# Gates of the first expert stage read from DRAM rows instead of selector products, with its first blocks moved ahead of the router's decision

## The reference: a decoder of two layers

```
# first expert stage: 2 shared and 16 routed experts, all computed for all tokens
h = relu(flat @ w1 + b1)                       # 18 experts of 176 hidden units
scores = sigmoid(flat @ centroids.T) + bias    # 16 routed experts
vals, idx = top_k(scores, 4)                   # gate of each token and expert,
gating = scattered(vals) / sum                 # 0 for twelve of the sixteen
out = flat + shared(h) + sum_e gating[:, e] * (h_e @ w2_e + b2_e)

# second expert stage: 32 experts with a capacity of 40 tokens each
Xp = x[slots_token]; Y = (silu(Xp @ Wg) * (Xp @ Wu)) @ Wd; out.at[slots_token].add(Y * w)
```

## Time and profile before

| | us |
|---|---|
| median of three runs | 715.11 (706.16 to 717.93) |
| the profiled execution's own time | 711.98 |
| its span in the profile | 710.1 |
| PE busy in the span | 615.1 (87%) |
| DVE, ACT, POOL busy | 396.7, 248.7, 328.3 |
| mean granted PE clock | 0.92 of full |

### The profile page before, as it was taken

The page is one execution under the profiler, slowest core; times in us unless marked ns, Lnnn a source line. Parts: engine busy times, 40 slices in busy tenths (PEclk is TensorE's granted clock), DMA queues, the critical chain, the costliest instruction groups (busy, mean ns, idle before and its releaser), DMA issues.

```text
span 710.1 us, 14147 instructions
## 1 busy us (share of the span) xinstructions
PE 615.1 (87%) x5509; PEld 384.1 (54%) x5509; DVE 396.7 (56%) x886; ACT 248.7 (35%) x554; POOL 328.3 (46%) x434
## 2 busy tenths in 40 slices
PE   5979989994989998899985998767999987897778
PEld 3435665442546665566652565533566655365467
DVE  3345755998437666556665565533476743943231
ACT  1214542003345443334441454321555553202340
POOL 2437726895347444444431876426688852200000
PEclk8989999996799998799998799995799999899999
DMA  6299262000200000000019895046000030016301
GB/s 227 76 170 261 66 267 113 0 1 0 76 1 0 1 1 1 1 0 2 1 56 152 108 116 182 0 104 104 2 3 3 2 135 2 1 32 243 131 26 60
DMA packets 23228, 48.41 MB, mean 68 GB/s; under 512 B 2569, under 2 KB 20507, under 8 KB 21115
## 3 DMA queue, kind: packets, MB, share of 16 engines
q1 hardware_dynamic: 21867, 44.92, 25.5%
q10 hardware_dynamic: 1296, 2.58, 1.0%
HBM read 39.63 MB, written 6.55 MB: 65 GB/s over the span
## 4 chain that ended last, share of the span: by engine, by line
PE 64%; DVE 15%; DMA 7%; POOL 4%; ACT 4%; issue 4%; SPq 3%; ACTq 0%; DVEq 0%; POOLq 0%
PE PS L1134 57%; PE PS L1138 4%; DVE R L958 3%; DVE R L955 3%; DMA R<-qk_scr 2%; SPq L330 2%; DMA WT<-in_wt_s_dram 2%; DVE stats L806 2%; DVE X L811 1%; PE PS L1157 1%; POOL R L476 1%; DMA X<-in_x_dram 1%; DVE xn L821 1%; POOL rstd L427 1%; ACT R L770 1%
## 5 line engine op out<-in xcount | busy, mean ns | idle before, releaser
L1134 PE MATMUL PS<-R 128*128 128x256 f16 (+5 forms) x2072 | 207.0, 271 | 0.1
L1134 PEld LDWEIGHTS PS<-R 128*128 128x128 f16 (+4 forms) x2072 | 135.3, 105 | 83.1 <-issue 51.8
L929 DVE TENSOR_REDUCE mx<-PS 128x4 bf16<-128x512 f32 x128 | 82.5, 686 | 53.1 <-PE PS L1134 53.1
L684 ACT ACTIVATE R<-PS 128x512 f32<-128x512 f32 x128 | 69.5, 595 | 102.5 <-PE PS L1134 102.5
L1134 PE MATMUL PS<-xnT,R 128*128 128x512 f16 (+1 forms) x348 | 87.2, 391 | 6.9 <-POOL R L555 5.4
L476 POOL TENSOR_TENSOR R<-mx,causal 128x512 bf16<-128x512 bf16 x64 | 65.2, 1040 | 54.2 <-DVE mx L929 53.5
L476 POOL TENSOR_TENSOR R<-mx,R 128x512 bf16<-128x512 bf16 x64 | 65.3, 1042 | 31.9 <-DVE mx L929 28.2
L553 POOL TENSOR_TENSOR R<-R 128x256 f16<-128x256 f32 (+1 forms) x50 | 35.3, 705 | 88.3 <-ACT R L723 88.3
L1004 DVE TENSOR_TENSOR R<-R,PS 128x512 f32<-128x512 f32 (+1 forms) x50 | 34.3, 686 | 58.2 <-ACT R L742 58.2
L1134 PEld LDWEIGHTS PS<-xnT,R 128*128 128x128 f16 (+1 forms) x348 | 34.8, 101 | 39.9 <-issue 10.1
L722 ACT ACTIVATE R<-R 128x256 f16<-128x256 f32 (+1 forms) x50 | 20.6, 413 | 84.9 <-PE PS L1134 84.9
(11 more groups left out here) (201 smaller groups left out, 889.7 us busy)
## 6 DMA issues: line engine op xcount, KB each, us to landing
R<-in_experts_dram SPq DMA_DIRECT2D x6, 1536.0 KB, 7.7
R<-qk_scr SPq DMA_DIRECT2D x48, 128.0 KB, 5.7
qk_scr<-R SPq DMA_DIRECT2D x16, 256.0 KB, 4.1
R<-in_w_dram SPq DMA_DIRECT2D x1, 3200.0 KB, 18.6
R<-in_w_dram SPq DMA_DIRECT2D x1, 3168.0 KB, 11.3
R<-qk_scr SPq DMA_DIRECT2D x48, 64.0 KB
R<-in_toe_dram SPq DMA_DIRECT2D x1, 2048.0 KB, 15.1
R<-in_experts_dram SPq DMA_DIRECT2D x2, 768.0 KB, 14.6
```

Of the source, the lines that this page charges most:

```text
L684: s.activation(PTm[:, u % 4, 4 * k:4 * k + 4, :], bank(2 + (2 * u + k) % 3).rearrange("p (h q) -> p h q", h=4), ACT.Exp, scale=c["sc"]).th ...
L929: v.tensor_reduce(mx[:, t % 4, 4 * k:4 * k + 4], bank(k).rearrange("p (h k) -> p h k", h=4), AX.X, ALU.max).then_inc(S("att_mx"), 1)
L1134: return nc.tensor.matmul(o_, l, r, start=start, stop=stop)
```

## The change

What it does, part by part:

- `sel`, `g3T`, the three bf16 parts and the gate product of every block are removed. The gates, turned once into `g0T` (18 rows of 1024), are stored to a DRAM scratch, and for each block with a routed expert (all but blocks 0 and 1, so 46 of the 50 steps) SP issues one to three transfers that read one row of 512 gates and write it to as many partitions as the block has of that expert, into a ring of four (`grow`). DVE multiplies in SBUF by SBUF.
- `up(0)`, `up(1)` stand ahead of the cross keys and of the wait for the gates; the values and `up(2)` follow the transposes; `keep_busy` is gone. High and low weights of blocks 0 and 1 are made before the layer norm's split, the bias products stand at the last block of a half, the hidden blocks have a ring of four, and the `flat` additions stand one each behind the low weights of blocks 4 to 11.
- ACT's casts of `wt_s1` in cross-attention stand at `t` = 16 and 20, POOL's subtractions at 18 and 22.
- In the second expert stage `expert_down` lags by one more group, the one-hots are turned one group ahead, and `dense_rows` stands two groups behind.

```diff
-            load(sel[0:96, :].bitcast(U16), A["sel"], "sel_ready")
+            for half in range(NH):
+                ts = slice(half * HF, (half + 1) * HF)
+                sp.wait_ge(S("g0T"), half + 1)
+                sp.dma_start(g_scr[:, ts], g0T[:, ts]).then_inc(S("g_parked"), 16)
+            sp.wait_ge(S("g_parked"), 16 * NH)
+            def gates(n):
+                i = GATED[n]
+                ts = slice(i // NB0 * HF, (i // NB0 + 1) * HF)
+                if n >= 4:
+                    sp.wait_ge(S("hg"), n - 3)
+                for e, lo, hi in gate_rows(i):
+                    sp.dma_start(grow[lo:hi, n % 4, :],
+                                 g_scr[e:e + 1, ts].broadcast_to([hi - lo, HF])).then_inc(S(f"grow{n % 4}"), 16)
+            for n in range(4):
+                gates(n)
...
+            for n in range(4, len(GATED)):
+                gates(n)

@@ gpsimd @@
-            for b in range(B):
-                flat(b)
-            for i in range(NH * NB0):
+            for i in range(2):
+                block_low(i)
...
+            for i in range(2, NH * NB0):
+                block_low(i)
+                if 4 <= i < 4 + B:
+                    flat(i - 4)

@@ scalar @@
+            for i in range(2):
+                block_high(i)
...
+            block_high(2)
...
             for i in range(NH * NB0):
+                if i == 2:
+                    cross_keys()
+                    gates()
...
-                if i >= 2:
-                    act.wait_ge(S("hg"), i - 1)
+                if i >= 4:
+                    act.wait_ge(S("hg16"), i - 3)

@@ vector @@
-                dve.wait_ge(S("gate_ps"), i + 1)
-                v.tensor_tensor(hg[0:m, i % 2, :], hid[0:m, i % 2, :], bank(2 + i % 2, parts=m),
-                                ALU.mult).then_inc(S("hg"), 1)
+                if i in GATED:
+                    n = GATED.index(i)
+                    dve.wait_ge(S(f"grow{n % 4}"), gates_loaded(n))
+                    h = hg[0:m, i % 2, :]
+                    v.tensor_tensor(h, hid[0:m, i % 4, :], grow[0:m, n % 4, :], ALU.mult).then_inc(S("hg"), 1)

@@ tensor @@
-            cross_keys()
-            keep_busy(24, 5)
-            pe.wait_ge(S("G3"), 1)
...
-                mm(bank(2 + i % 2, parts=m), sel[0:96, blk * P:blk * P + m], g3T[0:96, ts], True, True)
             up(0)
             up(1)
+            cross_keys()
+            pe.wait_ge(S("gf0"), 1)
...
+            cross_values()
+            pe.wait_ge(S("score0"), 1)
+            up(2)
...
+            down(0)
...
             expert_up(0)
+            turn_onehots(0)
             for gr in range(NGR):
                 if gr + 1 < NGR:
                     expert_up(gr + 1)
                 turn_hidden(gr)
-                turn_onehots(gr)
-                expert_down(gr)
+                if gr >= 1:
+                    expert_down(gr - 1)
+                turn_onehots(gr + 1)

@@ scalar, attention @@
-                    if c is CROSS and t in (4, 6):
+                    if c is CROSS and t in (16, 20):
                         act.wait_ge(S("w_s1"), 16)
```

More of the change, by code:

```diff
@@ L300, in pieces, with gate_rows, gates_loaded @@
             return 16 * sum(p_[0] // GE == gr for p_ in PIECES)
+        PLAIN = NS * FF // P
+        GATED = [i for i in range(NH * NB0) if i % NB0 >= PLAIN]
+        def gate_rows(i):
+            blk = i % NB0
+            first, last = blk * P, min(F0, (blk + 1) * P)
+            return [(e, max(first, e * FF) - first, min(last, (e + 1) * FF) - first)
+                    for e in range(NE0) if e * FF < last and (e + 1) * FF > first]
+        def gates_loaded(n):
+            return 16 * sum(len(gate_rows(GATED[k])) for k in range(n % 4, n + 1, 4))
         NGR = E1 // GE
@@ L698, in _, with block_high @@
                 s.activation(ub[:, b, :], xn[:, b, :], ACT.Copy, scale=skip[:, 0:1]).then_inc(S("xn_skip"), 1)
+            def block_high(i):
+                blk = i % NB0
+                m = P if blk < NB0 - 1 else LAST0
+                if i >= 4:
+                    act.wait_ge(S("down0"), i - 3)
+                s.activation(w1s[:, i % 4, 0, :, 0:m], W1[:, :, blk * P:blk * P + m], ACT.Copy).then_inc(S("w16_hi"), 1)
+                s.activation(w2s[0:m, i % 4, 0, :], W2[0:m, blk, :], ACT.Copy).then_inc(S("w16_hi"), 1)
+            act.wait_ge(S("w_e0"), 32)
+            act.wait_ge(S("conv_done"), DC * CH)
+            for i in range(2):
+                block_high(i)
             for b in range(4):
@@ L707, in _, with gates @@
                     weights_high("w16r", rw16[:, 0], rwT)
+            block_high(2)
             act.wait_ge(S("score0_ps"), 1)
             s.activation(rs0, bank(2, B * NR).rearrange("p (b e) -> p b e", b=B), ACT.Sigmoid).then_inc(S("score0"), 1)
-            cross_keys()
[L711 to L727, removed]
+            def gates():
+                for half in range(NH):
+                    act.wait_ge(S("g0T_ps"), half + 1)
+                    s.activation(g0T[:, half * HF:(half + 1) * HF], bank(4 + half, parts=NE0),
+                                 ACT.Copy).then_inc(S("g0T"), 1)
             for i in range(NH * NB0):
@@ L1218, in cross_keys, with cross_values @@
                     ins.then_inc(S("kx_ps"), 1)
+            def cross_values():
                 for b in range(B):
@@ L1449, in _ @@
             up(1)
-            for i in range(n0):
+            cross_keys()
+            pe.wait_ge(S("gf0"), 1)
+            for b in range(B):
+                ins = tr(PS[0:NE0, 4 + b // 4, b % 4 * P:(b % 4 + 1) * P], gf0[:, b, :])
+                if b % 4 == 3:
+                    ins.then_inc(S("g0T_ps"), 1)
+            cross_values()
+            pe.wait_ge(S("score0"), 1)
+            up(2)
+            pe.wait_ge(S("kx_lo"), NH)
+            pe.wait_ge(S("g0T"), NH)
+            down(0)
+            pe.wait_ge(S("vx"), 1)
+            pe.wait_ge(S("b_e0"), 16)
+            for i in range(1, n0):
                 if i + 2 < n0:
@@ L1631, in lay_out @@
                  np.zeros((1, D), np.float32)),
-        small=small, rows=rows, toe=toe, sel=sel.reshape(3 * GROUP, F0),
+        small=small, rows=rows, toe=toe,
         w1=w1.transpose(1, 0, 2).reshape(DC, P, F0).transpose(1, 0, 2),
```

112 lines of the change are left out of this document (45 added, 67 removed).

## The result

Median of 16 runs each: 704.18 us (697.57 to 712.32) with the change, 711.37 (706.16 to 718.47) before; ratio 0.9897, 95% interval 0.9866 to 0.9928. Some executions fall into a slower state: medians here are of all executions, ratios and intervals of the fast ones alone, so a ratio is not quite the quotient of the medians beside it. The profiled execution takes 703.65 us, with a span of 701.9 and a mean granted clock of 0.92.

What follows compares the result with a forecast made beforehand. PE was taken to bound the first expert stage, its steps 2.82 us. Terms 10.9 - 4.4 + 0 + 3.8 + 8.0 + 2.2 = 20.5 took 711.98 to 691.5; forecast 692, own range 684 to 699, full range 681 to 706.

Steps and rivals of the forecast that it cites:

- term of cross-attention: Start of cross-attention, units 5 to 8: three units fall from 16.2 to 8.2 us, 8.0 gained, upper end 8.8.
- second half: First expert stage: 24 steps give back 2.9 us, less 2.0 for biases, less some 0.9 of turns: 0.
- turns: First expert stage: DVE's SBUF-by-SBUF multiplication and POOL's subtractions hold each other for their duration less 0.14; step 2.70 us.
- Start: Start of the first expert stage: `down(0)` starts at 196.3 instead of 207.2, 10.9 us gained.
- First half: First expert stage, `down(0)` to `down(24)`: 70.1 us instead of 67.7, plus 2.0 for biases at its end; 4.4 lost.
- Change of halves: First expert stage: `down(25)` starts at 282.1 instead of 285.88, 3.8 us gained.
- lower end of 5: Cross-attention's gain is 5 us instead of 8.0 if the clock climbs later than it does now.
- Second expert stage: Shared groups: ACT bounds, groups with issues 4.4 to 5.0 us, the two without 3.9; 2.2 gained in all.
- Late parts give little: Rival: cross-attention gives 5, second expert stage 0, pauses under `flat` and `L454` lower PE's clock (3 lost); 700 us, chance 0.20.
- rivals on the turns (685, 716): First expert stage: no turns, step 2.61, 685 us, chance 0.10; turns for whole instructions, step 3.15, 716 us, chance 0.08.
- on the gate rows (729): Rival: gate-row transfers bound the first expert stage's multiplication; at 3.5 us a block 37 us lost, 729 us, chance 0.07.

Runs made afterwards that it cites:

- bias_first: The changed kernel with the eight bias products at the first block of each half, as before the change; 694.18 us against 712.91, ratio 0.974.
- psum_all: As `psum_hid`, with the product of hidden block and gate kept in PSUM too; 692.57 us, ratio 0.971 to the kernel before.
- psum_hid: The changed kernel with relu's result left in its PSUM bank, so DVE multiplies PSUM by SBUF; 693.53 us against 712.91 before, ratio 0.9735.

## Why the prediction was wrong, step by step

Three steps failed. The term of cross-attention put the whole fall of three units from 16.2 to 8.2 us down to one wait; the second half was put at 0, with turns and biases that both cost more there; and the preparation behind the stage had no term, though the moved biases pull PE's clock down ahead of it. In order of the sum:

- **Start**, 10.9 forecast, 13.0 measured. Right in mechanism: PE's order came as laid out, each group within 0.3 us of its term, but the eight transposes took 1.04 where I had put their bound of 1.99.
- **First half**, -4.4 forecast, -6.3 measured. The turns are what holds the step; the step of 2.70 is 2.75, those with `flat` 3.02 for 2.98, with the weights' subtraction 4.2 for 4.0. The bias products cost 2.9 and not 2.0: interleaved with the parts of the last `down`, they take longer than in a row.
- **Second half**, 0 forecast, -4.2 measured; the largest error in the first expert stage. "The second half's 24 steps give back 2.9" became 24 x 0.07 = 1.7; less 2.9 for the biases; less 1.4, since PE's pause under the four low parts grew from 2.70 to 4.08 (295.07) with the turns; less 0.6 at the last two blocks. Another 1.0 is a stretch at the lower clock at 294 to 298, in all three traces with the change and in two of the four before.
- **The preparation behind the stage**, no term, -2.7 measured. I moved the biases to the end of the half in the sum and asked what they take, not what PE's clock does behind them. `bias_first` gives it back.
- **Change of halves**, 3.8 forecast, 3.7 measured. Right.
- **Cross-attention**, 8.0 forecast, 2.9 measured; the largest error of all. The wait that the change removes is real, but one trace priced it, and that trace held the longest of six. Even there only 5.29 of the 16.2 us were PE's pause; that the three units would then take 8.2 also needs the clock up by then, which no wait of ACT decides: they took 9.54 at a granted clock of 0.72 in the changed kernel's trace, 7.7 to 12.6 over the eight without the wait. My lower end of 5 varied the clock alone, never the wait. Where the wait was about 4, in four traces, the stretch took 41.6, 41.7, 45.5 and 46.3, against 39.9 to 45.4 without it. So of the 2.9 some 1.7 are PE's pause, and the rest can be the chance of the clock.
- **Second expert stage**, 2.2 forecast, 1.0 measured. ACT bounds it as said: groups with issues take 4.5 to 6.1, not 4.4 to 5.0, and return what the quick ones gain.
- **Rivals.** "Late parts give little" (700) had the right direction and even the clock, but put the lower clock under `flat`, where none of the traces shows it, and had no loss in the second half. The rivals on the turns (685, 716) and on the gate rows (729) are out.

The differences sum to -13.1: 2.1 better at the start, then -1.9, -0.1, -4.2, -2.7, -5.1 and -1.2. My own range for the forecast, 684 to 699, let cross-attention vary by 3 and the second half not at all. The start came out 2.1 better than forecast, since its transposes had been put at an upper bound; that luck hid a part of the miss, which would have been 15.

## What to carry to other kernels

Before a product is replaced by data in SBUF, look where the operand lands: of the PE time saved (0.22 us a step) two thirds went to turns between DVE and POOL, and leaving the hidden block in PSUM brought it back without another instruction. Do not price the removal of a DMA wait by one trace, nor by the engine that waits: read how long the bounding engine pauses (0.2 to 1.0 us for waits of about 4), at which clock it runs there, and how both vary. And ask of every small product that is moved what PE's clock does behind it: eight narrow products cost 2.9 us where they stood and, at the end of the stage, about 2.7 more behind them.

## What the runs showed of the hardware that was not expected

- PE's clock fell to 1.2 GHz during or right behind a stretch of 4.2 us in which PE was busy without a pause, with eight products of 18 rows among twelve of 96. That was so in six of six traces at the end of the stage, but at the end of the first half in three of six.
- One transfer of 1024 KB of weights, issued at the same place in the program, released its reader 11.0 to 13.9 us later in six traces.
- A DVE cast from PSUM takes 0.69 us for 128x512 where one from SBUF takes 0.43, yet the kernel with it (`psum_all`) was no slower than `psum_hid`, and POOL's subtractions beside it stayed at 0.67.
- The second self-attention takes 86.7 to 97.5 us in 14 traces, and in eleven of them PE has pauses of 1.3 to 4.0 us that no instruction of another engine ends; in the three without, it takes 86.7 to 88.2. What starts them stays open.
